# Preparing the expert layer of a graph and mixture layer: slot one-hots in groups, one id map, scores behind it, three loads later, bias rows earlier

## The reference

```python
edge_index = jnp.stack([src, dst])
xn = _layernorm(x, axis=-1)
x = x + _L0_gnn_ref(xn, edge_index, ...) + _L0_mix_ref(xn[None], ...)[0]
x = x + _L0_ffn_ref(_layernorm(x, axis=-1)[None], ...)[0]
...
# _L0_gnn_ref: two graph attention layers (4 heads of 192, 2 heads of 96), then
combined = jnp.concatenate([x, out2], axis=-1)
return combined @ Wu + bu
...
# _L0_ffn_ref, 8 experts of 768 x 384 x 768, two for each node
gate = xt @ Wg + bg
scores, idx = jax.lax.top_k(gate, TOP_K)
h = jax.nn.gelu(jnp.einsum('td,edh->eth', xt, W1) + b1[:, None, :], approximate=False)
y = jnp.einsum('eth,ehd->etd', h, W2) + b2[:, None, :]
comb = jnp.sum(jax.nn.one_hot(idx, NUM_EXPERTS, dtype=x.dtype) * scores[..., None], axis=1)
out = jnp.einsum('te,etd->td', comb, y)
```

## Time and profile before

| | |
|---|---|
| median of 3 runs | 1147.48 us (1140.15 to 1147.85) |
| the profiled execution | 1146.19 us |
| its span in the profile | 1144.4 us |
| busy share of the span | PE 86%, DVE 66%, ACT 29%, POOL 8% |
| chain that ended last | PE 67%, DVE 18%, DMA 5%, issue 4%, ACT 3% |
| mean granted TensorE clock | 0.932 of full |

### The profile page before, as it was taken

How to read it: one execution, slowest core, us unless ns; L and a number is a source line. 1 busy time by engine, 2 the same in 40 slices (tenths; PEclk the granted TensorE clock), 3 DMA queues, 4 the chain that set the end, 5 groups by cost and what they waited for, 6 DMA issues and landing times.

```text
span 1144.4 us, 17088 instructions
## 1 busy us (share of the span) xinstructions
PE 984.6 (86%) x6386; PEld 709.4 (62%) x6388; DVE 755.2 (66%) x1711; ACT 335.8 (29%) x405; POOL 95.3 (8%) x113
## 2 busy tenths in 40 slices
PE   3699999989789899989898899778885399999991
PEld 3577777666454455457598899567753266666660
DVE  6576888877775687976698887699776612222221
ACT  3551112102014233333243333044444232222220
POOL 3000000000001000000000000000010223333321
PEclk9899999999899899999999999689996589999996
DMA  8341121252533556456691100041085135555536
GB/s 245 124 130 48 51 70 56 70 206 96 188 107 95 214 178 199 148 189 229 227 411 68 46 1 1 1 196 54 28 293 221 58 99 108 111 111 111 110 58 163
DMA packets 58522, 146.45 MB, mean 128 GB/s; under 512 B 11386, under 2 KB 30732, under 8 KB 55434
## 3 DMA queue, kind: packets, MB, share of 16 engines
q1 hardware_dynamic: 49514, 116.25, 29.2%
q0 software_dynamic: 6048, 21.24, 9.6%
q10 hardware_dynamic: 2880, 7.87, 1.7%
HBM read 95.94 MB, written 53.23 MB: 130 GB/s over the span
## 4 chain that ended last, share of the span: by engine, by line
PE 67%; DVE 18%; DMA 5%; issue 4%; ACT 3%; SPq 1%; DVEq 0%; POOLq 0%; ACTq 0%; POOL 0%
PE PS L1660 37%; PE PS L1909 12%; PE PS L1736 3%; DVE arena L1469 2%; DVE arena L1431 2%; DVE arena L1425 2%; PE PS L1985 2%; PE PS L2049 2%; PE PS L1747 1%; PE PS L1716 1%; PE PS L1751 1%; DMA xf_d<-arena 1%; DVE arena L1441 1%; DMA arena<-in_L_gnn_W_dram 1%; DVE arena L1331 1%
## 5 line engine op out<-in xcount | busy, mean ns | idle before, releaser
L1660 PE MATMUL PS<-arena 128*128 128x384 f16 (+6 forms) x3276 | 552.9, 322 | 12.3 <-ACT arena L1040 8.8
L1660 PEld LDWEIGHTS PS<-arena 128*128 128x128 f16 (+1 forms) x3276 | 309.8, 99 | 215.6 <-issue 12.2
L1909 PE MATMUL PS<-arena 128*128 128x193 f32 (+1 forms) x1200 | 190.5, 322 | 21.7 <-DVE arena L1431 16.8
L1909 PEld LDWEIGHTS PS<-arena 128*128 128x128 f32 x1200 | 186.2, 199 | 25.9 <-DVE arena L1431 15.6
L987 ACT ACTIVATE arena<-arena,AS 128x1280 f32<-128x1280 f32 x60 | 81.8, 1363 | 132.2 <-DVE arena L1425 132.0
L1650 DVE TENSOR_SCALAR arena<-PS,arena 128x768 f32<-128x768 f32 x27 | 27.5, 1018 | 139.8 <-PE PS L2075 139.8
L1425 DVE SCALAR_TENSOR_TENSOR arena<-arena,AS 128x1280 f32<-128x1280 f32 x60 | 92.7, 1548 | 0.0
L1431 DVE SCALAR_TENSOR_TENSOR arena<-arena 128x1280 f32<-128x1280 f32 x60 | 89.4, 1490 | 4.8 <-PE PS L1909 4.8
L1233 DVE TENSOR_SCALAR arena<-arena 128x240 f16<-128x240 f16 x324 | 90.4, 279 | 0.0
L1232 DVE TENSOR_SCALAR arena<-arena 128x128 f16<-128x128 f16 x324 | 81.3, 251 | 0.4 <-DMA b2c<-in_L_gnn_b_dram 0.4
L1063 ACT ACTIVATE arena<-PS 128x1536 f16<-128x1536 f16 x27 | 39.2, 1450 | 108.4 <-PE PS L2049 108.4
(11 more groups left out here) (268 smaller groups left out, 945.8 us busy)
## 6 DMA issues: line engine op xcount, KB each, us to landing
arena<-in_L_ffn_W_dram SPq DMA_DIRECT2D x48, 384.0 KB, 4.1
fr_d<-arena SPq DMA_DIRECT2D x48, 384.0 KB, 3.3
arena<-fr_d SPq DMA_DIRECT2D x16, 1152.0 KB, 14.8
arena<-in_x_dram SPq DMA_DIRECT2D x18, 384.0 KB, 5.2
arena<-rr_d SPq DMA_DIRECT2D x4, 1280.0 KB, 8.1
acc_d<-arena SPq DMA_DIRECT2D x11, 384.0 KB, 2.6
g_d<-arena SPq DMA_DIRECT2D x10, 388.0 KB, 2.3
acc_d<-arena ACTq DMA_DIRECT2D x10, 384.0 KB, 5.6
```

What stands on the lines that cost most here:

```text
L1660: m = T.matmul(out, left[i][x], right[i][y], start=first and i + r == 0, stop=last and 3 * i + r == n - 1)
L1909: m = T.matmul(ps[b][:, r * (C + 1):(r + 1) * (C + 1)], PT[i % deep][:, d * P:(d + 1) * P], feats, start=t == 0 and r == 0, stop=t == NT - ...
```

## The change

The groups for ranks and one-hots are now three, tiles 0 to 4, 5 to 7, and 8 and 9. For each, `ohslot` is made by one instruction from the low seven bits of the rank, before the number of slot tiles is known. The id is one f16 value, so that the first chain of matmuls has 27 columns; the three score maps are made on VectorE behind the list and brought to their slots by a second chain of 81 columns, behind the first `up`. `rows_in(1)` uses another pair of PSUM banks. The `late` loads also wait until eight tiles have their low halves. The bias rows are cleared and loaded in layer two and split at the start of the tile stage. The three loads of sums for the tile stage stand together.

```diff
-        NQ = 5
+        NQ = 3
...
-        ohslot = big(0, NS * P // 2).bitcast(BF16).rearrange("p (k n) -> p k n", k=NS)
+        ohslot = reg(O_X, NS * P // 2).bitcast(F16).rearrange("p (k n) -> p k n", k=NS)
...
+        GROUPS = ((0, HALFT), (HALFT, NT - 2), (NT - 2, NT))
+        GATE_BANK = (4, 5, 4)
+        RANK_BANK = (6, 7, 5)
...
+        def rows_bank(i):
+            return 5 if i == 1 else 0
...
             for u in masked:
                 experts(u)
+            sp.wait_ge(s_fbs_blank, 2)
+            for r in (0, 64, 96):
+                sp.dma_start(fbs[r:r + NE, 0:HID], fb1).then_inc(s_fbs_in, 16)
...
             sp.wait_ge(s_fin_psum, NT)
             sp.wait_ge(s_bias_high, 3)
+            sp.wait_ge(s_rown_ready, NT - 2)
             for u in late:
                 experts(u)
...
-            pool.wait_ge(s_o2t_psum, 9)
-            pool.wait_ge(s_head_out, 5 * (H1 + H2))
+            pool.wait_ge(s_t2_ready, (H1 + 1) * NT)
+            pool.wait_ge(s_agg, H1 * NT)
+            pool.wait_ge(s_max_done, (H1 + H2) * NT)
             g.memset(out2T[KS:KS + 1, 0:NP], 1.0).then_inc(s_fbs_blank, 1)
...
-                if s in (6, 7):
-                    bias_rest(s - 6)
+                if s == 1:
+                    bias_rest(1)
...
+            def spread_slots(q, low):
+                dve.wait_ge(s_dve_step, low)
+                s = slots_of(q)
+                n = s.stop - s.start
+                high = mark(V.tensor_tensor(hi128[:, s], rankf[:, s], lowf[:, s], ALU.subtract))
+                V.tensor_tensor(ohslot[:, s, :], seqh.rearrange("p (a n) -> p a n", a=1).to_broadcast([P, n, P]),
+                                lowf[:, s].rearrange("p (k a) -> p k a", a=1).to_broadcast([P, n, P]), ALU.is_equal).then_inc(s_ohslot_ready, 1)
+                return high
+
+            def all_rank_parts(q):
+                dve.wait_ge(s_rank_psum, q + 1)
+                spread_slots(q, low_part(q, low_bits(q, rank_int(q, rank_sum(q, rank_products(q))))))
...
+            dve.wait_ge(s_rown_ready, NT)
+            dve.wait_ge(s_x2_out, 16 * NT)
+            all_rank_parts(0)
+            chosen(1)
+            chosen(2)
+            all_rank_parts(1)
+            dve.wait_ge(s_rank_psum, 3)
...
-            for k in range(NS):
-                V.tensor_scalar(ohslot[:, k, :], seqb, partf[:, 1, k:k + 1], None, ALU.is_equal).then_inc(s_ohslot_ready, 1)
...
+            link(V.tensor_scalar(empty, ps[6][:, 0:NTL], 0.0, dumpf, ALU.is_equal, ALU.mult))
+            V.scalar_tensor_tensor(found, ps[6][:, 0:NTL], -1.0, empty, ALU.add, ALU.add).then_inc(s_found_ready, 1)
...
             rows_in(0)
+            rows_in(1)
...
+                else:
+                    pe.wait_ge(s_map_scores, NQ)
+                    for k in range(NS):
+                        m = T.matmul(ps[7][:, 0:NQ * NTL].rearrange("p (q i) -> p q i", q=NQ), ohslotb[:, k, :], maps[:, :, k, :], start=k == 0, stop=k == NS - 1)
+                    m.then_inc(s_map_psum, 1)
```

More of the change, by code:

```diff
@@ L239, in rt @@
             return small(TE).rearrange("p (t e) -> p t e", t=NT)
-        gate, slotm, top8 = rt(), rt(), rt()
+        gate, top8 = rt(), rt()
         idx8 = rt().bitcast(U32)
-        idxf = rt()
-        O12 = small(2 * TE).rearrange("p (c t e) -> p c t e", c=2, t=NT)
+        idxf = small(NS)
+        O12 = small(2 * TE).rearrange("p (k e) -> p k e", k=NS)
         OSh = small(TE // 2).bitcast(F16).rearrange("p (t e) -> p t e", t=NT)
@@ L248, in gps_layer @@
         cet = small((NE + 1) * NE).rearrange("p (f e) -> p f e", e=NE)
-        ohtile = low(5 * D, NS * NTL).rearrange("p (k i) -> p k i", k=NS)
+        MAPW = NS * NTL // 2
+        ohtile = low(5 * D, MAPW).bitcast(F16).rearrange("p (k i) -> p k i", k=NS)
+        mapid = low(5 * D + MAPW, MAPW).bitcast(F16).rearrange("p (k i) -> p k i", k=NS)
+        OR = low(5 * D + 2 * MAPW, 2 * TE).rearrange("p (k e) -> p k e", k=NS)
+        assert 2 * MAPW + 2 * TE <= D
         wg = small(KC * NE).rearrange("p (k e) -> p k e", k=KC)
@@ L256, in gps_layer @@
         eint = small(NTL).bitcast(I32)
[L257 to L260, removed]
+        rankf, hi128, base, tilef = (small(NS) for _ in range(4))
+        ranki, lowi, idi = (small(NS).bitcast(I32) for _ in range(3))
+        lowf = small(NS // 2).bitcast(F16)
+        idh = small(NS // 2).bitcast(F16)
         vals = v3(small(NQ * NS), NQ)
@@ L271, in gps_layer @@
         seqi = small(P).bitcast(I32)
-        seqb = small(P // 2).bitcast(BF16)
+        seqh = small(P // 2).bitcast(F16)
         pidx = small(1)
@@ L1513, in _, with mark, chosen @@
             seq8 = seq[:, 0:NE].rearrange("p (a e) -> p a e", a=1)
-            def chosen(a, b):
+            def mark(ins):
+                chain[0] += 1
+                ins.then_inc(s_dve_step, 1)
+                return chain[0]
+            def chosen(q):
+                a, b = GROUPS[q]
                 n = b - a
                 dve.wait_ge(s_gate_psum, b)
-                link(V.scalar_tensor_tensor(gate[:, a:b, :], ps[(4, 7)[a // HALFT]][:, a * NE:b * NE].rearrange("p (t e) -> p t e", t=n), 1 / UP,
+                link(V.scalar_tensor_tensor(gate[:, a:b, :], ps[GATE_BANK[q]][:, a * NE:b * NE].rearrange("p (t e) -> p t e", t=n), 1 / UP,
                                             bgrow.rearrange("p (a e) -> p a e", a=1).to_broadcast([P, n, NE]), ALU.mult, ALU.add))
@@ new lines, in slots_of, with rank_sum, rank_int, low_bits @@
+            def slots_of(q):
+                a, b = GROUPS[q]
+                return slice(2 * a, 2 * b)
+            def rank_sum(q, products):
+                dve.wait_ge(s_dve_step, products)
+                return mark(V.tensor_reduce(rankf[:, slots_of(q)], OR[:, slots_of(q), :], axis=AX.X, op=ALU.add))
+            def rank_int(q, sums):
+                dve.wait_ge(s_dve_step, sums)
+                return mark(V.tensor_copy(ranki[:, slots_of(q)], rankf[:, slots_of(q)]))
+            def low_bits(q, ints):
+                dve.wait_ge(s_dve_step, ints)
+                return mark(V.tensor_single_scalar(lowi[:, slots_of(q)], ranki[:, slots_of(q)], P - 1, op=ALU.bitwise_and))
```

227 lines of the change are left out of this document (124 added, 103 removed).

## The result

The changed kernel takes 1128.26 us (median of 4 runs, 1125.28 to 1128.78) against 1145.77 us (4 runs, 1140.15 to 1147.85): a ratio of 0.985, with a 95% interval of 0.981 to 0.989. It was run again in two of the groups of experiments: 0.985 (0.982 to 0.987) and 0.986 (0.983 to 0.990). The direction held, the size did not: the gain is 16 to 17.5 us, and my sum had 13.4. The profiled execution took 1128.78 us with a span of 1127.0. The last layer-two row of VectorE stands at 821.88 in both profiles, so their times can be compared directly up to there.

The account below looks back on a forecast made before the run. TensorE was taken as the bound, with 67% of the chain. Terms 0.4 - 6.6 - 7.6 - 0.8 + 1.2 = -13.4 us gave 1132.8 from the profile or 1134.1 from the median; forecast 1133.5 us, range 1129 to 1140.

Parts of the forecast that it names:

- Late loads and bias rows: Tile stage: late loads waiting for eight low halves gain 6.6 us, moving the bias rows costs 0.4 us.
- Last gates to gather: Preparation between the last gates and the first gather: 10.0 us against 17.6, a term of -7.6 us.
- Behind the gather: From gather to first `up`: `up` can start when ScalarE's first copy ends, -0.8 us.
- Score chain: 20 matmuls of 81 columns behind the first `up`, where TensorE has no gap: +1.2 us.
- The loop: The loop after the preparation: TensorE's own and unchanged, so no term in the sum.
- TensorE's gaps keep their places, moved by half a microsecond: Tile stage: the argument against a low clock that begins with step 4 or 5 and stays.
- rival 4's fast side: TensorE's clock: the low stretch is missed, total 1130 us; chance 0.06.
- rivals 1 and 2: Stall moves to `row_high(9)`, 1140 us, chance 0.13; gather waits for the last store, 1135 to 1137 us, chance 0.07.
- the order of completions: Transfers: a completion is written only after the engine's earlier writes, so stores behind the late loads land when those end.
- Rival 3: Preparation on VectorE: wide one-hots are dear, 5 us in all against 2.9, total 1135.5 us; chance 0.08.
- rival 4's slow side: TensorE's clock: low level begins with step 4 or 5 and stays, total 1147 to 1150 us; chance 0.04.

Follow-up runs that it names:

- before_filler: The kernel before with 20 idle matmuls behind the last rank and 20 behind the map: 1140.27 us, ratio 0.997.
- scores_ahead: The changed kernel with score maps made before VectorE's wait for the id map and score products right behind that map: 1131.84 us.

## Why the prediction was wrong in size

Means of the four profiles of before and the three of after, against my terms:

- *Late loads and bias rows, -6.2.* From the last reciprocal to the first `fin` 8.02 to 7.41, from there to the last gates 64.01 to 57.38: **-7.2**. By itself the wait gave -6.1 and, taken away, +7.0. The stall that went averages 6.5 us, and nothing took its place. The rest, -0.7, stands against +0.4 for the bias rows. That term's steps were right where the clock was the same; what it lacked is what the low clock does to the rest of the stage. No total here tells the move's worth from nothing.
- *Last gates to gather, -7.6.* 17.62 to 9.85, within 0.02 us in every profile of the table: **-7.8**. The three one-hots were priced within 0.1 us each by the row of equal size.
- *Behind the gather, -0.8.* 8.48 to 7.56: **-0.9**. The second gather's landing, not the copy, is what `up` now waits for (0.48 us in front of the transposes at 903.80).
- *Score chain, +1.2.* 4.70 to 4.99: **+0.3**. The products cost 0.9, mis-sized by 0.3; the rest is that the first `up` itself took 4.70 before and 4.09 after, by the clock.
- *The loop, 0.* 197.82 to 196.39: **-1.4**. The period is the same; in three of four profiles of before the last tile fell into a low stretch, in none of the three of after. Over all profiles it was three of seven with the old preparation and one of eleven with the new.

Together -17.1, which agrees with the 16.2 and 17.5 of the runs. **The step that failed is the clock.** "TensorE's gaps keep their places, moved by half a microsecond" put its term at nothing in the sum, and rival 4's fast side had 0.06 of the chance and 1130 as its time. Of the 3.7 us beyond the sum, 2.0 are the clock's in `up` and the last tile, 1.0 lies in the tile stage, whose length goes with the places of the low clock, and 0.6 are small errors of the other terms. The earlier trace rows showed an `up` with most of its time at the lower level; a term for what the clock can return there was due, of 0 to 1.8 us, and more for the tile stage, and the range ought to have reached to 1126.

How much of this the change itself brings is open. In the first pair of profiles `up` and the last tile give 3.4 us, in these means 2.0, and over the 16 profiles without idle matmuls in front of `up` only some 1. That the last gates stood at 887.91, against 887.5 forecast, was luck: `fin` ran partly at the lower level there, and before it did not.

I also took one profile as the kernel's typical one. The forecast of 1133.5 starts from 1146.19 and 1147.48 us, while the 56 timed runs of the kernel before in the result and the first three groups have a median of 1144.0. Some 2 to 3 of the 5.2 us between forecast and measurement are this start, and the rest is the sum.

What I had of rivals: rivals 1 and 2 did not happen (no transfer released a `row_high` or the gather); the late loads' traffic ended at 893 to 894 (the window 893:894 has a DMA share of 0.36), the list came at 896.9, so the order of completions was not put to the test. Rival 3 did not happen either. Of rival 4's slow side the low clock came, under the first `fin` and again from 847.5, but it did not stay, and none of 15 runs was slower than before.

The parts alone gained 6.1, 11.2 and 2.2 us, which is 2 to 3 more than the whole. With stages that move by 6 us from one execution to the next, and 5 to 18 runs of each, that is within what they can tell; I have no run that settles it. Whether the last tile's low stretch belongs to the kernel before or was chance stays open too.

The Trainium skill, "TensorE: Matmul & The Clock Gate", section "What's actually happening", says that for modelling the ramp costs less than 1% of a typical kernel's span and shouldn't be fitted to a particular number of slow matmuls. The traces agree with both: 6 us of 1144 in the tile stage, in places that don't repeat. But the change was worth 1.5%, so half of one per cent was a third of the answer, and it needed a range where it could have no fixed term.

## What to carry to other kernels

Before an edit of a few microseconds is priced, take more than one profile of the kernel before and write its stages side by side: what differs between them is the error of every term that is read from one. Where a chain leaves TensorE idle in front of work that it bounds, give the clock a term and a range of its own. Idle matmuls in TensorE's gaps may pay where its work follows at once (3.2 us less in total with them in the tile stage, with overlapping intervals); 5.1 us in front of `up` they left it at 5.34 us, and 3.9 us in front of it at 3.09.

## What was not expected of the hardware

- The same kernel's tile stage took 60.85, 63.53, 64.12 and 67.55 us in four executions, by the places of the low clock alone and 1.4 us of difference in the stall. The executions with the low clock under the first `fin` tiles were the long ones.
- A store of 384 KB, issued behind three loads of 1152 KB, held ScalarE for 5.1 to 7.2 us in nine profiles; held back by one line, the loads held up nothing that the profiles show, though they ran beside three more stores.
- The first `up`, eighteen matmuls of the same shapes, took from 3.09 us (`before_filler`) to 5.43 us (`scores_ahead`).
